# Softmax attention of a two-layer kernel: VectorE takes the maximum of a pair of products ahead of the low part of the weights in each slot

## The chip, the cores and the metric

The program runs on one core of a Trainium2 chip. The metric is the device time of one execution in microseconds (us), as the median over the runs. The profile is of one execution on that core.

## What is computed

The reference chains a linear attention, a mixture of 16 experts, a softmax attention and a mixture of 64 experts over two sequences of 2048 tokens of 256 features, all in float32. The change touches the softmax attention alone. Cut to that:

```python
h = layernorm(x); c_q, c_kv = h @ w_down_q.T, h @ w_down_kv.T
q, k, v = (heads of c_q @ w_up_q.T, c_kv @ w_up_k.T, c_kv @ w_up_v.T)   # 2 x 16 heads, 2048 x 64
q, k = rope(q), rope(k)
scores = jnp.einsum('bhqd,bhkd->bhqk', q, k) / 8
attn = jax.nn.softmax(scores, axis=-1)
out = jnp.einsum('bhqk,bhkd->bhqd', attn, v)
```

## The kernel before

The stages run one after the other, with a barrier between them; `softmax_attention` is one of them. It works through 32 heads (16 pairs of two), each in 32 **slots**. Slot n of a head is a quarter of the queries (512) against 256 keys. Eight slots (`PER`) make one quarter of the queries.

Operands of TensorE are float32 numbers in a rounded format (fp32r). To keep accuracy, each factor is split into a high and a low part. So there are these pieces of work, each with its own engine and its own queue, whose order is written out by hand:

- **TensorE** (`head`, from L1644), in slot n: first the *scores* of slot n+2 (4 matmuls, L1621 and L1622), then the *products* of slot n+13 (2 matmuls into `ps_u`, L1606; `PAHEAD` is 13), then the *values* of slot n (6 matmuls, L1638 to L1640, twice three). Products are a first look at the scores of a later slot, only for their maximum. They wait until the maximum before has been read out of `ps_u` (semaphore `u_max`), since there is one buffer. The values of slot n wait for the low parts of slot n (`pl_ready` from VectorE for the first half of the tile, `pl2_ready` from GpSimd for the second).
- **ScalarE** takes the exponential of the scores twice, into `pf` (float32, L1572) and `ph` (rounded, L1573).
- **GpSimd** (`low_part`, L1440) takes `pl = pf - ph` for the second half of each tile, and in slots 16 to 23 of a head splits the next head's values (`vh` L1427, `vl` L1433, in turn).
- **VectorE** takes `pl = pf - ph` for the first half (`low_part`, L1503), takes the maximum over the pair of products (`maxima`, L1485), and once in 8 slots, after the maximum of slots 2, 10, 18 and 26, makes the softmax's stabilising row of a quarter of the queries (`stabilisers`, L1490, L1495 and L1497, all of four elements per partition). In slots 7, 9, 11 and 13 it also splits q and k of the next head: a bit mask (`cut_low`, L1471) ahead of the maximum and a subtraction (`take_low`, L1478) behind it. The last head has no head after it, so it splits nothing.

VectorE's low part in slot n is that of slot n+1, and its maximum that of slot n+13. Below, L(k), M(k), G(k) and V(k) stand for VectorE's low part, its maximum, GpSimd's low part and the start of the values of slot k. GpSimd's G(k+1) and VectorE's L(k+1) are both released by the same exponential of slot k+1.

The waits of the parts:

```python
dve.wait_ge(s["p_ready"], g * SLOTS + (n + 3))        # low_part(g, n): exponential of slot n
dve.wait_ge(s["u_full"], base * SLOTS + (j + 1))      # maxima: products of slot j
pe.wait_ge(s["u_max"], base * SLOTS + j)              # products: the maximum before
pe.wait_ge(s["pl_ready"], g * SLOTS + (n + 1))        # values, first half
```

Of the kernel before, what the change touches and what calls it, by code (L numbers as in the profile page):

```python
# [133 lines left out]
class Kernel:  # L134
# [1145 lines left out]
    def softmax_attention(self):  # L1280
# [3 lines left out]
        SLOTS = NQB * KC // 2  # L1284
# [7 lines left out]
        with ctx:  # L1292
# [172 lines left out]
            @block.vector  # L1465
            def _(dve):
                def cut_low(base, hh, half, i):

                    if i == 0:
                        dve.wait_ge(s[f"raw{hh}"], half * 32 + 32)  # L1470
                    dve.tensor_scalar(cut[:, i % 2], raw[hh][:, i * QB:(i + 1) * QB].bitcast(U32), KEEP, None,  # L1471
                                      ALU.bitwise_and).then_inc(s["cut_ready"], 1)

                def take_low(base, hh, i):
                    dve.wait_ge(s["cut_ready"], base * NQB + (i + 1))
                    if i > 1 or not isinstance(base, int) or base > 0:
                        dve.wait_ge(s[f"low{i % 2}"], base * 64 + 32 * (i // 2))
                    dve.tensor_tensor(low[:, i % 2], raw[hh][:, i * QB:(i + 1) * QB].bitcast(F32),  # L1478
                                      cut[:, i % 2].bitcast(F32), ALU.subtract).then_inc(s["low_ready"], 1)

                def maxima(base, hh, j):

                    qb, i = j // PER, j % PER
                    dve.wait_ge(s["u_full"], base * SLOTS + (j + 1))
                    dve.tensor_reduce(mx[:, qb % 2, 2 * i:2 * i + 2], ps_u[:], X, ALU.max).then_inc(s["u_max"], 1)  # L1485

                def stabilisers(base, hh, j):
                    qb = j // PER
                    dve.wait_ge(s["u_max"], base * SLOTS + (j + 1))
                    dve.tensor_reduce(mg[:], mx[:, qb % 2].rearrange("p (t k) -> p t k", k=4), X, ALU.max)\  # L1490
                        .then_inc(s["mg_ready"], 1)
                    if not isinstance(base, int) or base > 0:
                        dve.wait_ge(s[f"row{qb}"], base * 32)
                    dve.wait_ge(s["mg_ready"], base * NQB + (qb + 1))
                    dve.tensor_scalar(nmh[:, qb], mg[:], -1.0, None, ALU.mult).then_inc(s["own"], 1)  # L1495
                    dve.wait_ge(s["own"], base * NQB + (qb + 1))
                    dve.scalar_tensor_tensor(nml[:, qb], mg[:], -1.0, nmh[:, qb].bitcast(F32), ALU.mult, ALU.subtract)\  # L1497
                        .then_inc(s["nm_ready"], 1)

                def low_part(g, n):  # L1500
                    dve.wait_ge(s["p_ready"], g * SLOTS + (n + 3))
                    at = slice(0, QB)
                    dve.tensor_tensor(pl[:, n % NP, at], pf[:, n % NP, at], ph[:, n % NP, at].bitcast(F32), ALU.subtract)\  # L1503
                        .then_inc(s["pl_ready"], 1)

                def head(pr, hh, prepare):
                    g = pr * 2 + hh
                    nxt = pr * 2 + (hh + 1)
                    for n in range(SLOTS):
                        if n + 1 < SLOTS or prepare:  # L1510
                            low_part(g, n + 1)
                        i = n - 7
                        cutting = prepare and 0 <= i < 2 * NQB and i % 2 == 0
                        if cutting:
                            cut_low(nxt, 1 - hh, pr + hh, i // 2)
                        j = n + PAHEAD
                        if j < SLOTS:
                            maxima(g, hh, j)
                        elif prepare:
                            maxima(nxt, 1 - hh, j - SLOTS)  # L1520
                        if cutting:
                            take_low(nxt, 1 - hh, i // 2)
                        if j % PER == PER - 1:
                            if j < SLOTS:
                                stabilisers(g, hh, j)
                            elif prepare:
                                stabilisers(nxt, 1 - hh, j - SLOTS)

                dve.wait_ge(s["fixed"], 4)
                for i in range(NQB):  # L1530
                    cut_low(0, 0, 0, i)
                    take_low(0, 0, i)
                for j in range(PAHEAD):
                    maxima(0, 0, j)
                    if j % PER == PER - 1:
                        stabilisers(0, 0, j)
                low_part(0, 0)
                for pr in range(PAIRS - 1):
                    head(pr, 0, True)
                    head(pr, 1, True)  # L1540
                head(PAIRS - 1, 0, True)
                head(PAIRS - 1, 1, False)

# [288 lines left out]
```

## Time and profile before

| | |
|---|---|
| time, median of 3 runs | 5355.44 us (5354.14 to 5355.58) |
| the profiled execution's own time | 5353.76 us |
| its span | 5351.6 us |
| TensorE busy in the span | 4242.4 us (79%) |
| VectorE | 3795.4 us (71%) |
| GpSimd | 2569.8 us (48%) |
| ScalarE | 2514.5 us (47%) |
| mean granted clock of TensorE | 0.887 |

The profiled execution's own time is 2.2 us longer than its span, and 1.7 us under the median. Shares of the span average over stages with different limits, so they do not say what bounds the attention. The attention's values run from 1355.7 us to 4265.5 us of the span, over half of it. A busy TensorE is not TensorE at its peak: matmuls overlap, so a gap between two starts can be hidden in their lengths, and the distance between starts is the better measure.

### The profile page before, as it was taken

What the parts mean: (1) busy time and instruction counts of PE and PEld (TensorE: products, weight loads), DVE (VectorE), ACT (ScalarE), POOL (GpSimd) and SP (SyncE); (2) the same over time, 40 slices, a digit from 0 to 9 for tenths busy, and PEclk for the clock granted to TensorE, in tenths of its full rate; (3) what the DMA queues carried; (4) which work ended last, traced back from release to release, by engine and by line L of the source; (5) the groups of instructions that cost most, each with busy time, mean ns of one, the idle gap of its engine ahead of it and who ended that gap; (6) DMA issues with size and microseconds to landing.
All of it is one profiled execution on the core that took longest, in us unless ns stands there. A gap on an engine that the chain in (4) does not pass through costs nothing. (4 is left out here: it accounts for less than half of the span.)

```text
span 5351.6 us, 60841 instructions
## 1 busy us (share of the span) xinstructions
PE 4242.4 (79%) x17953; PEld 3145.6 (59%) x17954; DVE 3795.4 (71%) x5546; ACT 2514.5 (47%) x3236; POOL 2569.8 (48%) x2320
## 2 busy tenths in 40 slices
PE   7963577674999999999999999999999845411274
PEld 5652243353777777777777777777777734311132
DVE  6755344474899999999999999999999712355322
ACT  2211111232677777777777777777777600000011
POOL 0003466365455555555555555555555500166664
PEclk8875899787999999999999999999999967755597
DMA  9022223366223232322223232323232166300366
GB/s 96 11 82 76 34 46 46 118 237 195 56 50 70 50 70 50 69 50 60 58 51 67 46 71 48 70 50 70 50 70 50 32 110 102 94 11 11 76 186 182
DMA packets 489984, 397.34 MB, mean 74 GB/s; under 512 B 225145, under 2 KB 428174, under 8 KB 477216
## 3 DMA queue, kind: packets, MB, share of 16 engines
q1 hardware_dynamic: 456992, 369.14, 30.7%
q0 software_dynamic: 32768, 25.44, 3.0%
q8 instruction: 113, 1.85, 0.1%
q14 instruction: 111, 0.91, 0.1%
HBM read 247.83 MB, written 116.75 MB: 68 GB/s over the span
## 5 line engine op out<-in xcount | busy, mean ns | idle before, releaser
L1440 POOL TENSOR_TENSOR at_pl<-at_pf,at_ph 128x512 fp32r<-128x512 f32 x1024 | 1430.1, 1397 | 1307.6 <-ACT at_ph L1573 1307.5
L1572 ACT ACTIVATE at_pf<-at_ps_s 128x1024 f32<-128x1024 f32 x1024 | 1051.4, 1027 | 789.4 <-PE at_ps_s L1622 786.6
L1485 DVE TENSOR_REDUCE at_mx<-at_ps_u 128x2 f32<-128x1024 f32 x1024 | 1243.1, 1214 | 156.8 <-PE at_ps_u L1606 156.8
L1503 DVE TENSOR_TENSOR at_pl<-at_pf,at_ph 128x512 fp32r<-128x512 f32 x1024 | 1202.1, 1174 | 71.5 <-ACT at_ph L1573 68.7
L1573 ACT ACTIVATE at_ph<-at_ps_s 128x1024 fp32r<-128x1024 f32 x1024 | 1046.9, 1022 | 0.0
L1622 PE MATMUL at_ps_s<-at_q,at_k 66*128 66x512 f32 x2048 | 818.4, 400 | 0.0
L1638 PE MATMUL at_ps_v<-at_ph,at_vh 128*128 128x512 f32 x2048 | 815.1, 398 | 0.2 <-POOL at_pl L1440 0.2
L1621 PE MATMUL at_ps_s<-at_q,at_k 128*128 128x512 f32 x2048 | 813.1, 397 | 0.3 <-ACT at_ph L1573 0.3
L1640 PE MATMUL at_ps_v<-at_pl,at_vh 128*128 128x512 f32 x2048 | 811.8, 396 | 0.0
L1639 PE MATMUL at_ps_v<-at_ph,at_vl 128*128 128x512 f32 x2048 | 803.6, 392 | 0.0
L730 POOL DMA_INDIRECT table<-rt_entry,rt_slot x320 | 316.9, 990 | 988.6 <-DVE rt_entry L626 521.8
L1606 PE MATMUL at_ps_u<-at_k,at_qp 128*128 128x512 f32 x2048 | 668.9, 408 | 68.9 <-DMA at_q<-at_low 45.3
L1606 PEld LDWEIGHTS at_ps_u<-at_k,at_qp 128*128 128x128 f32 x2048 | 373.3, 191 | 227.1 <-DVE at_mx L1485 107.2
L1622 PEld LDWEIGHTS at_ps_s<-at_q,at_k 66*128 66x128 f32 x2048 | 387.8, 189 | 94.8
L1640 PEld LDWEIGHTS at_ps_v<-at_pl,at_vh 128*128 128x128 f32 x2048 | 385.8, 188 | 97.1
L1621 PEld LDWEIGHTS at_ps_s<-at_q,at_k 128*128 128x128 f32 x2048 | 388.4, 190 | 91.5 <-ACT at_ph L1573 1.0
L1639 PEld LDWEIGHTS at_ps_v<-at_ph,at_vl 128*128 128x128 f32 x2048 | 384.4, 188 | 93.7
L1638 PEld LDWEIGHTS at_ps_v<-at_ph,at_vh 128*128 128x128 f32 x2048 | 385.0, 188 | 85.5 <-POOL at_pl L1440 0.6
L713 PE MATMUL rt_ps_p<-rt_mask,tri 128*128 128x16 bf16 (+1 forms) x64 | 13.7, 214 | 431.3 <-DVEq L606 313.2
L1723 PE MATMUL op_ps_o<-op_wo,op_oT 128*128 128x256 f32 x512 | 180.2, 528 | 188.5 <-DVE x_sb L1740 143.2
L713 PEld LDWEIGHTS rt_ps_p<-rt_mask,tri 128*128 128x128 bf16 x64 | 6.7, 104 | 456.3 <-DVEq L606 331.3
L1723 PEld LDWEIGHTS op_ps_o<-op_wo,op_oT 128*128 128x128 f32 x512 | 138.7, 278 | 230.0 <-DVE op_oT L1734 200.5
(217 smaller groups left out, 5230.7 us busy)
## 6 DMA issues: line engine op xcount, KB each, us to landing
at_k<-kT SPq DMA_DIRECT2D x64, 512.0 KB
at_q<-qT SPq DMA_DIRECT2D x64, 512.0 KB
ex_wgu<-Wgu_in SPq DMA_DIRECT2D x64, 384.0 KB
qT<-pj_rot SPq DMA_DIRECT2D x32, 512.0 KB, 3.1
vT<-pj_vo SPq DMA_DIRECT2D x32, 512.0 KB, 4.4
kT<-pj_rot SPq DMA_DIRECT2D x32, 512.0 KB, 3.1
at_raw<-qT SPq DMA_DIRECT2D x32, 512.0 KB, 4.7
at_raw<-kT SPq DMA_DIRECT2D x32, 512.0 KB, 6.6
```

Source lines behind the costliest of these rows:

```text
L1440: pool.tensor_tensor(pl[:, n % NP, at], pf[:, n % NP, at], ph[:, n % NP, at].bitcast(F32), ALU.subtract).then_inc(s["pl2_ready"], 1)
L1485: dve.tensor_reduce(mx[:, qb % 2, 2 * i:2 * i + 2], ps_u[:], X, ALU.max).then_inc(s["u_max"], 1)
L1503: dve.tensor_tensor(pl[:, n % NP, at], pf[:, n % NP, at], ph[:, n % NP, at].bitcast(F32), ALU.subtract)\
L1572: act.activation(pf[:, n % NP], ps_s[:, n % 2], ACT.Exp, scale=DH ** -0.5)
L1573: act.activation(ph[:, n % NP], ps_s[:, n % 2], ACT.Exp, scale=DH ** -0.5)\
L1606: m = pe.matmul(ps_u[:, w], tile, k1[hh][:, kb * QB:(kb + 1) * QB], start=True, stop=True)
L1621: pe.matmul(out, k1[hh][:, ks], q1[hh][:, qs], start=True, stop=False)
L1622: m = pe.matmul(out, k2[hh][0:MROW + 2, ks], q2[hh][0:MROW + 2, qs], start=False, stop=True)
L1638: pe.matmul(out, vh[:, hh, c], ph[:, n % NP, keys], start=c == 0, stop=False)
L1639: pe.matmul(out, vl[:, hh, c], ph[:, n % NP, keys], start=False, stop=False)
L1640: m = pe.matmul(out, vh[:, hh, c], pl[:, n % NP, keys], start=False, stop=c == KC - 1)
L1723: m = pe.matmul(ps_o[:, r % 2, 0:D], oT[:, r, g], wo[:, g], start=g == 0, stop=g == G - 1)
```

## The change

The two lines that issue VectorE's low part of the next slot move from the head of the slot to behind the maximum. No instruction is added or removed, and no wait is changed. Of the other instructions of a slot, the bit mask (L1471) stays ahead of the maximum, and the subtraction (L1478) and the stabilising row stay behind, now behind the low part too.

```diff
                     for n in range(SLOTS):
-                        if n + 1 < SLOTS or prepare:
-                            low_part(g, n + 1)
                         i = n - 7
                         cutting = prepare and 0 <= i < 2 * NQB and i % 2 == 0
                         if cutting:
...
                             maxima(g, hh, j)
                         elif prepare:
                             maxima(nxt, 1 - hh, j - SLOTS)
+                        if n + 1 < SLOTS or prepare:
+                            low_part(g, n + 1)
                         if cutting:
                             take_low(nxt, 1 - hh, i // 2)
                         if j % PER == PER - 1:
```

VectorE's queue, slots 7, 8 and 9 of the second head, before:

```order
L1503 TENSOR_TENSOR at_pl<-at_pf,at_ph 128x512
L1471 TENSOR_SCALAR at_cut<-at_raw 128x512
L1485 TENSOR_REDUCE at_mx<-at_ps_u 128x2
L1478 TENSOR_TENSOR at_low<-at_raw,at_cut 128x512
L1503 TENSOR_TENSOR at_pl<-at_pf,at_ph 128x512
L1485 TENSOR_REDUCE at_mx<-at_ps_u 128x2
L1503 TENSOR_TENSOR at_pl<-at_pf,at_ph 128x512
L1471 TENSOR_SCALAR at_cut<-at_raw 128x512
L1485 TENSOR_REDUCE at_mx<-at_ps_u 128x2
L1478 TENSOR_TENSOR at_low<-at_raw,at_cut 128x512
```

The same three slots after the change:

```order
L1471 TENSOR_SCALAR at_cut<-at_raw 128x512
L1485 TENSOR_REDUCE at_mx<-at_ps_u 128x2
L1503 TENSOR_TENSOR at_pl<-at_pf,at_ph 128x512
L1478 TENSOR_TENSOR at_low<-at_raw,at_cut 128x512
L1485 TENSOR_REDUCE at_mx<-at_ps_u 128x2
L1503 TENSOR_TENSOR at_pl<-at_pf,at_ph 128x512
L1471 TENSOR_SCALAR at_cut<-at_raw 128x512
L1485 TENSOR_REDUCE at_mx<-at_ps_u 128x2
L1503 TENSOR_TENSOR at_pl<-at_pf,at_ph 128x512
L1478 TENSOR_TENSOR at_low<-at_raw,at_cut 128x512
```

The low part of slot n+1 has moved behind the mask and the maximum, and stands directly ahead of the subtraction.

VectorE's queue, slot 18 and the start of slot 19 of the second head, before:

```order
L1503 TENSOR_TENSOR at_pl<-at_pf,at_ph 128x512
L1485 TENSOR_REDUCE at_mx<-at_ps_u 128x2
L1490 TENSOR_REDUCE at_mg<-at_mx 128x4
L1495 TENSOR_SCALAR at_nmh<-at_mg 128x4
L1497 SCALAR_TENSOR_TENSOR at_nml<-at_mg,at_nmh 128x4
L1503 TENSOR_TENSOR at_pl<-at_pf,at_ph 128x512
L1485 TENSOR_REDUCE at_mx<-at_ps_u 128x2
```

The same place after the change:

```order
L1485 TENSOR_REDUCE at_mx<-at_ps_u 128x2
L1503 TENSOR_TENSOR at_pl<-at_pf,at_ph 128x512
L1490 TENSOR_REDUCE at_mg<-at_mx 128x4
L1495 TENSOR_SCALAR at_nmh<-at_mg 128x4
L1497 SCALAR_TENSOR_TENSOR at_nml<-at_mg,at_nmh 128x4
L1485 TENSOR_REDUCE at_mx<-at_ps_u 128x2
L1503 TENSOR_TENSOR at_pl<-at_pf,at_ph 128x512
```

Behind the three small instructions of the row now comes a maximum, where a low part came before. TensorE's queue is the same in both kernels, and so are those of the other engines.

## Rows read from the trace of the kernel before

**Rows 1.** Busy time and clock, by stretch: the whole attention.

```profile
core 0: us, PE busy (x) PEld busy (x) DVE busy (x) ACT busy (x) POOL busy (x), PEclk, DMA share, GB/s
1355.00:4267.00 2912.00, 2903.55 (x12251) 2293.70 (x12249) 2682.28 (x2663) 2162.48 (x2296) 1641.16 (x1271) 1.00 0.25 56
```

**Rows 2.** TensorE in time, slot 7 of the 15th head.

```profile
start us, us, engine line op out<-in xcount [idle before <-releaser]
...
2652.94 0.39 PE L1621 MATMUL at_ps_s<-at_q,at_k 128*128 128x512 f32 x1
2653.17 0.40 PE L1622 MATMUL at_ps_s<-at_q,at_k 66*128 66x512 f32 x1
...
2653.88 0.63 PE L1606 MATMUL at_ps_u<-at_k,at_qp 128*128 128x512 f32 x2
2654.35 0.40 PE L1638 MATMUL at_ps_v<-at_ph,at_vh 128*128 128x512 f32 x1
```

**Rows 3.** The values' line L1638 from the 15th head's start to the 16th's.

```profile
L1638 PE MATMUL at_ps_v<-at_ph,at_vh x65: 391/397/400, 2634.7 to 2725.9; 128*128 128x512 f32 x65
```

**Rows 4.** The page's costliest groups: maximum, both low parts.

```profile
L1440 POOL TENSOR_TENSOR at_pl<-at_pf,at_ph 128x512 fp32r<-128x512 f32 x1024 | 1430.1, 1397 | 1307.6 <-ACT at_ph L1573 1307.5
...
L1485 DVE TENSOR_REDUCE at_mx<-at_ps_u 128x2 f32<-128x1024 f32 x1024 | 1243.1, 1214 | 156.8 <-PE at_ps_u L1606 156.8
L1503 DVE TENSOR_TENSOR at_pl<-at_pf,at_ph 128x512 fp32r<-128x512 f32 x1024 | 1202.1, 1174 | 71.5 <-ACT at_ph L1573 68.7
```

**Rows 5.** VectorE in time, the 15th head's slots 1 and 2 and behind.

```profile
2636.40 0.69 DVE L1503 TENSOR_TENSOR at_pl<-at_pf,at_ph 128x512 fp32r<-128x512 f32 x1 [0.29 <-ACT at_ph L1573]
2637.70 1.23 DVE L1485 TENSOR_REDUCE at_mx<-at_ps_u 128x2 f32<-128x1024 f32 x1 [0.60 <-PE at_ps_u L1606]
...
2642.24 1.23 DVE L1497 SCALAR_TENSOR_TENSOR at_nml<-at_mg,at_nmh 128x4 fp32r<-128x4 f32 x1
2643.40 0.68 DVE L1503 TENSOR_TENSOR at_pl<-at_pf,at_ph 128x512 fp32r<-128x512 f32 x1
2644.00 1.21 DVE L1485 TENSOR_REDUCE at_mx<-at_ps_u 128x2 f32<-128x1024 f32 x1
2645.13 1.67 DVE L1503 TENSOR_TENSOR at_pl<-at_pf,at_ph 128x512 fp32r<-128x512 f32 x1
```

**Rows 6.** GpSimd in time, the 15th head's slots 0 to 9.

```profile
2636.55 1.70 POOL L1440 TENSOR_TENSOR at_pl<-at_pf,at_ph 128x512 fp32r<-128x512 f32 x1 [1.10 <-ACT at_ph L1573]
...
2642.16 1.29 POOL L1440 TENSOR_TENSOR at_pl<-at_pf,at_ph 128x512 fp32r<-128x512 f32 x1 [1.10 <-ACT at_ph L1573]
2644.97 1.28 POOL L1440 TENSOR_TENSOR at_pl<-at_pf,at_ph 128x512 fp32r<-128x512 f32 x1 [1.51 <-ACT at_ph L1573]
...
2653.39 1.29 POOL L1440 TENSOR_TENSOR at_pl<-at_pf,at_ph 128x512 fp32r<-128x512 f32 x1 [1.49 <-ACT at_ph L1573]
2656.20 1.28 POOL L1440 TENSOR_TENSOR at_pl<-at_pf,at_ph 128x512 fp32r<-128x512 f32 x1 [1.51 <-ACT at_ph L1573]
2659.01 1.28 POOL L1440 TENSOR_TENSOR at_pl<-at_pf,at_ph 128x512 fp32r<-128x512 f32 x1 [1.52 <-ACT at_ph L1573]
```

**Rows 7.** Who waited for VectorE's maximum, L1485.

```profile
  PEld at_ps_u L1606: 107.2, 231
```

**Rows 8.** VectorE in time, slots 7 to 9 of the 15th head.

```profile
2655.16 0.41 DVE L1471 TENSOR_SCALAR at_cut<-at_raw 128x512 uint32<-128x512 uint32 x1
2655.49 1.21 DVE L1485 TENSOR_REDUCE at_mx<-at_ps_u 128x2 f32<-128x1024 f32 x1
2656.63 1.40 DVE L1478 TENSOR_TENSOR at_low<-at_raw,at_cut 128x512 fp32r<-128x512 f32 x1
```

**Rows 9.** VectorE in time, two neighbours that meet GpSimd, in another head.

```profile
1558.71 0.69 DVE L1503 TENSOR_TENSOR at_pl<-at_pf,at_ph 128x512 fp32r<-128x512 f32 x1 [0.29 <-ACT at_ph L1573]
1559.32 1.52 DVE L1471 TENSOR_SCALAR at_cut<-at_raw 128x512 uint32<-128x512 uint32 x1
```

**Rows 10.** GpSimd in time, the same stretch.

```profile
1558.86 1.70 POOL L1440 TENSOR_TENSOR at_pl<-at_pf,at_ph 128x512 fp32r<-128x512 f32 x1 [0.99 <-ACT at_ph L1573]
```

**Rows 11.** Lines with shapes kept apart: GpSimd's split of the values' low part.

```profile
L1433 POOL TENSOR_TENSOR at_vl<-at_vf,at_vh 128x256 fp32r<-128x256 f32 x124 | 134.3, 1083 | 0.0
```

## The prediction

> **What bounds the kernel now.** I first read the busy time by stretch: in the attention TensorE is busy 2903.55 of 2912 us at a granted clock of 1.00, the upper of its two levels (2.4 GHz) [rows 1]. The chain of waits has nothing to say of this stage, so I went to the order of instructions in time. In [rows 2] the starts of neighbouring matmuls are 0.23 us apart, and from the first scores' matmul (2652.94) to the values (2654.35) there are six of them in 1.41 us, 0.235 each. The reader is to see that this is TensorE's own pace: no gap is left. A slot has 12 matmuls; the values of slot 0 to slot 7 of that head start from 2634.7 [rows 3] to 2654.35, so 2.81 us a slot. I take 2.805.
>
> Then I looked for what lies above this pace. From one head's first value matmul to the next's it is 2725.9 - 2634.7 = 91.2 us [rows 3], while 32 slots of 2.805 are 89.8. So **1.4 us a head are lost to stalls**, some 45 us over 32 heads: this is all that any reordering in this stage can win. The waits name the loser: the weight load of the products waits for VectorE's maximum 231 times, 107.2 us in sum [rows 7]. (Some of that is hidden, since weights load ahead of time.)
>
> Why is VectorE late, at 1.21 us for a maximum and 0.69 for a low part, in a slot of 2.8? Because the low part takes 1174 ns on average, not 690 [rows 4]. The two timelines side by side show it. At 2636.40 L starts, G starts behind it at 2636.55 and takes 1.70, until 2638.25, which is 1.16 after L's end [rows 5, 6]. At 2644.97 G is first and takes its own 1.28; L, started at 2645.13, ends at 2646.80, 0.55 behind G [rows 5, 6]. So two subtractions of these engines do not run together: **the one that starts second ends 0.56 us behind GpSimd, or 1.15 us behind VectorE**. The maximum, which reads PSUM, is never held: 1214 ns on average [rows 4]. The tiny L1497 is held too: 1.23 us at 2642.24, until GpSimd's end at 2643.45 [rows 5, 6].
>
> **The change, step by step.** Instructions, durations and semaphores are the same; only who meets whom changes, and what the values wait for. I give times from V(n), the start of values in slot n.
>
> *A quiet slot.* G(n+2) starts at V(n)+1.85: 2656.20 against 2654.35 [rows 2, 6]. The maximum of slot n+13 can start at V(n)+0.20 (2637.70 [rows 5] against 2634.7+2.8) and takes 1.21 to 1.23. So the low part of slot n+1, now behind it, starts at V(n)+1.35 (neighbours overlap by 0.08, as 2643.40 + 0.68 and 2644.00 in [rows 5]) and ends at V(n)+2.04. It is needed at V(n)+2.805: on time by 0.75. It also starts 0.50 ahead of GpSimd, and GpSimd has 2.8 us until its half is needed, so that being held costs it nothing. A quiet slot stays at TensorE's pace, and gain and loss there are zero. What covers this is that half microsecond.
>
> *When the maximum starts more than 0.50 late.* Then G is first. It ends at V(n)+1.85+1.29, the low part 0.56 later, the values start some 0.06 behind: V(n)+3.76 in place of V(n)+2.805. **Each such low part costs TensorE 0.95 us**, a step and not a slope. The old order had the low part done a whole slot ahead, so only the maximum's own lateness cost anything.
>
> *Slots 7 to 9.* I walk the new queue in the times of the 15th head. L(7) runs 2652.87 to 2653.56; G, released at 2653.39 [rows 6], waits and ends at 2653.56 + 1.15 = 2654.71. The mask (0.41 alone [rows 8]) asks at 2653.48 and is held until 2655.00. The maximum follows, 2654.92 to 2656.13, and L(8) starts at 2656.05, before G at 2656.20 [rows 6]: in time, ends 2656.74. G now ends at 2657.89. The subtraction L1478 stands directly behind L(8), and is held until 2657.89 + 0.56 = 2658.45. The maximum of slot 8 could have started at 2657.35 and starts at 2658.37, over a microsecond late, and ends at 2659.58: products wait 0.15. L(9) comes at 2659.50, behind G at 2659.01 [rows 6], and ends at 2659.01 + 1.29 + 0.56 = 2660.86. V(9) was due at 2654.35 + 2 x 2.805 = 2659.96 and starts near 2660.92. Stall: 0.96 in all.
>
> *That GpSimd gets in between* is the link that decides. The trace has it: L starts at 1558.71 [rows 9], G at 1558.86 [rows 10]; the mask asks at 1559.32 with no gap behind L [rows 9], and yet G ends at 1560.56 [rows 10], 1.16 behind L, and the mask only at 1560.84 [rows 9].
>
> *The other slots.* The stall gives VectorE 0.95 us, and the backlog builds again. In slot 10 the row's small instructions are held by G(12), the mask of slot 11 comes behind them, its maximum starts 0.92 late, and L(12) meets G: 0.95 at slot 12. The same happens behind the mask and subtraction of slot 13, at L(15), by a margin of only 0.12 us. In slots 16 to 23 GpSimd also splits values, 1083 ns for the low part of a piece [rows 11]; in slot 18 L1497 is held by it, the maximum of slot 19 starts 0.3 late and slot 20's low part misses G by 0.26: a fourth stall. In slots 2 and 26 the row's instructions cost the next maximum some 0.3, under the 0.50: no stall.
>
> Sum: 4 x 0.95 = 3.8 us a head, less the 1.4 of today, whose cause (low parts held in a row, then a late maximum) mostly goes. That is +2.4 us in 31 heads (the last one splits nothing): **+73 us**. Against the profiled execution's own 5353.76 that is 5427; it lies 1.7 under the median, so 5428. Bounds: with the two sure stalls alone (slots 9 and 12) the sum is 1.9 - 1.4 = +0.5 a head, +15 us, 5370; with a fifth, 4.75 - 1.4 = +3.35, +104 us, 5459. I take four, since the walk finds four, the nearest rows being those of the same slots.
>
> The rows give 0.55 between GpSimd's end and that of a held low part whose free length is 0.69, so a part of the work goes on while it is held. The Trainium skill (SBUF — State Buffer, section "SBUF: two separate sides" and the one behind it) has VectorE and GpSimd share a port pair that the first holds for its whole instruction while the other fully blocks, and gives about 115 ns on top of the other's end before the blocked one runs. Taken at its word, a late low part would end 0.69 + 0.115 behind G, some 0.25 later than by the rows, which over 4 x 31 is 30 us more, 5458 (an estimate from that page and these counts). Rows come first.
>
> **Rivals.**
>
> 1. *Faster, 5312.* VectorE keeps its place against GpSimd between neighbours, and the backlog disappears. Without GpSimd in between, L1478 of slot 7 would end at 2657.35, the maximum of slot 8 would start on time at 2657.35, and L(9) at 2658.48, ahead of G at 2659.01. All 1.4 us of today's stalls would go as well, since low parts at 0.69 in place of 1174 ns [rows 4] free VectorE: 31 x 1.4 = 43 us less. It decides if the low part's start stays under V(n)+1.85. For it speaks that quiet slots are surely better off; against it [rows 9, 10]. 9%.
> 2. *No change.* The stalls only change hands: one new stall of 0.95 and some short ones in place of the 1.4. It needs the mask of slot 7 or the subtraction not to be held. 5350 to 5365. 5%.
> 3. *Slower, but by little.* Two stalls a head: the later ones hang on margins of 0.12 and 0.26. 5370 to 5395. 20%.
> 4. *The forecast*, three to five stalls: 5400 to 5460. 64%, and 2% for more.
>
> **How the numbers follow.** The measurement can tell about 0.2%, 11 us. Faster is rival 1, 0.09; same is rival 2, 0.05; the rest, 0.86, is slower. The predicted time is that of the likeliest case, 5428. The range takes in cases 3 and 4, 5370 to 5460.
>
> **What would show it.** In the changed profile: maxima as long as before (1.21), low parts shorter on average (about 0.85 us), GpSimd's longer; TensorE's values at L1638 now wait for VectorE's low part L1503, which is nearly absent today, about 4 times a head near slots 9, 12, 15 and 20 with gaps of 0.8 to 0.95; the products' waits for the maximum nearly gone; one head at 93 to 94 us in place of 91.2. The forecast is wrong if the low part at slot 9 starts ahead of GpSimd's, or if a head takes 90 us. Stages ahead of 1355 us and behind 4267 us must not move.

## The result, and the profile after

The change makes the kernel slower: 5444.59 us (median of 4 runs, 5442.53 to 5447.85) against 5355.51 us (4 runs, 5354.14 to 5355.82). The ratio is 1.0167, with a 95% interval of 1.015 to 1.0185; that is 89 us more.

The busy time of the attention, with its columns as in [rows 1], and the page's costliest groups, as in [rows 4], after the change:

```profile
1354.00:4350.00 2996.00, 2910.29 (x12251) 2285.07 (x12249) 2415.12 (x2663) 2163.94 (x2295) 1550.01 (x1271) 1.00 0.25 54
```

```profile
L1440 POOL TENSOR_TENSOR at_pl<-at_pf,at_ph 128x512 fp32r<-128x512 f32 x1024 | 1381.8, 1349 | 1483.5 <-ACT at_ph L1573 1483.4
L1485 DVE TENSOR_REDUCE at_mx<-at_ps_u 128x2 f32<-128x1024 f32 x1024 | 1249.7, 1220 | 565.3 <-PE at_ps_u L1606 565.0
...
L1503 DVE TENSOR_TENSOR at_pl<-at_pf,at_ph 128x512 fp32r<-128x512 f32 x1024 | 904.0, 883 | 19.4 <-ACT at_ph L1573 19.4
L1638 PE MATMUL at_ps_v<-at_ph,at_vh 128*128 128x512 f32 x2048 | 831.0, 406 | 85.7 <-DVE at_pl L1503 85.5
```

The attention is 84 us longer at the same granted clock of 1.00, and VectorE is busy there for 267 us **less** than in [rows 1]: its low part takes 883 ns in place of 1174. An average like this would speak for the change. The last row is what costs: TensorE's values now wait for VectorE's low part, 85.5 us in sum, a line that before had no such entry. That this sum is so near the loss is chance. It counts the idle time alone, 0.70 us at each of 122 waits, while the starts of the values move by 0.94 us there and by another 0.10 in the next slot: 129 us in all, from which the 44 us of the old stalls go. The maximum costs less in exchange: the products' weight load waits for it 104 times in place of 231, 49.7 us in sum in place of 107.2.

```profile
  PEld at_ps_u L1606: 49.7, 104
```

One head, the 15th, from its first value matmul to the next head's (the values' line, as in [rows 3]), and who waits for VectorE's low part over the whole run:

```profile
L1638 PE MATMUL at_ps_v<-at_ph,at_vh x65: 390/397/503, 2671.0 to 2765.0; 128*128 128x512 f32 x65
```

```profile
who waited for it (us, times):
  PEld at_ps_v L1638: 156.0, 216
  PE at_ps_v L1638: 85.5, 122
```

94.0 us a head in place of 91.2, and 122 waits of TensorE: four in each of the 31 heads that have one after them would be 124. In this head they are at slots 9, 12, 15 and 20, by the distances between the starts of values: 3.75 us in place of 2.81 at each.

Now the place where it happens. VectorE, GpSimd and TensorE in time, slots 7 to 9 of that head (columns: start, duration, engine, instruction, idle time before it in brackets):

```profile
2689.14 0.68 DVE L1503 TENSOR_TENSOR at_pl<-at_pf,at_ph 128x512 fp32r<-128x512 f32 x1
2689.74 1.52 DVE L1471 TENSOR_SCALAR at_cut<-at_raw 128x512 uint32<-128x512 uint32 x1
2691.18 1.21 DVE L1485 TENSOR_REDUCE at_mx<-at_ps_u 128x2 f32<-128x1024 f32 x1
2692.31 0.68 DVE L1503 TENSOR_TENSOR at_pl<-at_pf,at_ph 128x512 fp32r<-128x512 f32 x1
2692.91 1.78 DVE L1478 TENSOR_TENSOR at_low<-at_raw,at_cut 128x512 fp32r<-128x512 f32 x1
2694.61 1.21 DVE L1485 TENSOR_REDUCE at_mx<-at_ps_u 128x2 f32<-128x1024 f32 x1
2695.74 1.36 DVE L1503 TENSOR_TENSOR at_pl<-at_pf,at_ph 128x512 fp32r<-128x512 f32 x1
```

```profile
2689.65 1.32 POOL L1440 TENSOR_TENSOR at_pl<-at_pf,at_ph 128x512 fp32r<-128x512 f32 x1 [1.49 <-ACT at_ph L1573]
2692.46 1.68 POOL L1440 TENSOR_TENSOR at_pl<-at_pf,at_ph 128x512 fp32r<-128x512 f32 x1 [1.49 <-ACT at_ph L1573]
2695.27 1.29 POOL L1440 TENSOR_TENSOR at_pl<-at_pf,at_ph 128x512 fp32r<-128x512 f32 x1 [1.13 <-ACT at_ph L1573]
```

```profile
2695.88 0.73 PE L1606 MATMUL at_ps_u<-at_k,at_qp 128*128 128x512 f32 x2
2697.16 0.50 PE L1638 MATMUL at_ps_v<-at_ph,at_vh 128*128 128x512 f32 x1 [0.55 <-DVE at_pl L1503]
2697.50 0.40 PE L1639 MATMUL at_ps_v<-at_ph,at_vl 128*128 128x512 f32 x1
2697.74 0.39 PE L1640 MATMUL at_ps_v<-at_pl,at_vh 128*128 128x512 f32 x1
```

The low part of slot 8 (2692.31) is ahead of GpSimd's (2692.46) by 0.15 us. The subtraction behind it is held (1.78 in place of 0.68), the next maximum is late, and slot 9's low part (2695.74) comes 0.47 behind GpSimd's start (2695.27). It ends at 2697.10, and the values start at 2697.16. The last two rows show something the prediction did not have: from the late matmul to the next are 0.34 us and not 0.23.

### The profile page after: what moved, and what is told of

The parts are those of the page before. It is cut to its first block and busy times, and to the rows that moved or that the text cites. A ratio compares the mean times of both kernels' runs of the same rounds, so it can differ in the third digit from the quotient of the medians.

```text
span 5445.8 us, 60841 instructions
## 1 busy us (share of the span) xinstructions
PE 4257.3 (78%) x17953; PEld 3142.5 (58%) x17954; DVE 3528.5 (65%) x5546; ACT 2517.0 (46%) x3236; POOL 2478.2 (46%) x2320
## 5 line engine op out<-in xcount | busy, mean ns | idle before, releaser
L1440 POOL TENSOR_TENSOR at_pl<-at_pf,at_ph 128x512 fp32r<-128x512 f32 x1024 | 1381.8, 1349 | 1483.5 <-ACT at_ph L1573 1483.4
L1485 DVE TENSOR_REDUCE at_mx<-at_ps_u 128x2 f32<-128x1024 f32 x1024 | 1249.7, 1220 | 565.3 <-PE at_ps_u L1606 565.0
L1503 DVE TENSOR_TENSOR at_pl<-at_pf,at_ph 128x512 fp32r<-128x512 f32 x1024 | 904.0, 883 | 19.4 <-ACT at_ph L1573 19.4
L1638 PE MATMUL at_ps_v<-at_ph,at_vh 128*128 128x512 f32 x2048 | 831.0, 406 | 85.7 <-DVE at_pl L1503 85.5
L1606 PE MATMUL at_ps_u<-at_k,at_qp 128*128 128x512 f32 x2048 | 655.3, 401 | 61.0 <-DMA at_q<-at_low 45.1
L1638 PEld LDWEIGHTS at_ps_v<-at_ph,at_vh 128*128 128x128 f32 x2048 | 384.6, 188 | 237.2 <-DVE at_pl L1503 156.0
L1606 PEld LDWEIGHTS at_ps_u<-at_k,at_qp 128*128 128x128 f32 x2048 | 384.2, 192 | 180.1 <-DVE at_mx L1485 49.7
```

The lines of the kernel that those rows point to most:

```text
L1440: pool.tensor_tensor(pl[:, n % NP, at], pf[:, n % NP, at], ph[:, n % NP, at].bitcast(F32), ALU.subtract).then_inc(s["pl2_ready"], 1)
L1606: m = pe.matmul(ps_u[:, w], tile, k1[hh][:, kb * QB:(kb + 1) * QB], start=True, stop=True)
L1638: pe.matmul(out, vh[:, hh, c], ph[:, n % NP, keys], start=c == 0, stop=False)
```

## The experiments

Four theories. **A**: the low part is late where VectorE's maximum starts over 0.50 us late, because GpSimd's low part is then first and holds it, a step of 0.95 us or more. **B**: VectorE has too much work around slots 7 to 15, and a low part behind the maximum is late whoever it meets. **C**: the new order costs something in every slot. **D**: lateness adds up smoothly, without a step. C and D come up at the runs that speak of them.

The kernels ran in two groups of four, on two chips, on which the kernel before took 5351.6 us (first group) and 5310.2 us (second group); each is compared with its own group. The expectations were written as times against 5355.5 us for the kernel before and 5444.6 us for the new order, so the difference to the kernel before is what counts. The new order itself was not run again in these groups; where a kernel is compared with it, its 89 us and its stretch are those of the first measurement. "Stretch" is the time from the first to the last start on the values' line. It was 2909.8 us before and is 2994.6 us after the change, and it is free of what the stages ahead and behind do.

| kernel | median, us | against before, us | ratio (95%) | stretch, us |
|---|---|---|---|---|
| new order, GpSimd waits for L(k-1) | 5325.19 | -26 | 0.9948 (0.9931 to 0.9964) | 2882.6 |
| old order, GpSimd waits for L(k) | 5304.3 | -47 | 0.9912 (0.9896 to 0.9929) | 2864.9 |
| new order, GpSimd narrow | 5303.77 | -48 | 0.9906 (0.989 to 0.9923) | 2864.1 |
| old order in slots 7 to 15 | 5380.1 | +29 | 1.0054 (1.0037 to 1.0071) | 2936.5 |
| new order, split one slot later | 5363.94 | +54 | 1.0101 (1.0084 to 1.0118) | 2962.7 |
| new order, tiny mask and subtraction | 5328.88 | +19 | 1.0031 (1.0021 to 1.0042) | 2929.4 |
| old order, GpSimd narrow (one run) | 5270.03 | -40 | none | 2865.9 |
| new order, two added delays | 5415.3 | +105 | 1.0197 (1.018 to 1.0214) | 3011.4 |

### New order, with GpSimd's low part kept behind VectorE's

```diff
 def low_part(g, n):                       # GpSimd
     pool.wait_ge(s["p_ready"], g * SLOTS + (n + 3))
     stand_alone(pool, s["turns"])
+    if g * SLOTS + n > 0:
+        pool.wait_ge(s["pl_ready"], g * SLOTS + n)
+        stand_alone(pool, s["turns"])
```

> The new order, and GpSimd's low part of slot k starts only when VectorE's low part of slot k-1 is done, so that VectorE is never the second at the place where it came late. Theory A (the low part is late because it meets GpSimd's, which was first): the four stalls of 1.04 us a head shrink to two short ones, near slots 12 and 20, about 0.7 us a head in all; 5335 us. VectorE's low part then takes 0.69 us on average in place of 0.88. Theory B (VectorE has too much work in slots 7 to 15, and the low part behind the maximum is late whoever it meets): the added wait can only delay; 5445 us or more.

26 us faster than before, where 20 were expected, and so some 115 us faster than the new order without the wait. Adding a wait to GpSimd, and nothing else, took the loss away. Who waits for VectorE's low part now:

```profile
L1506 DVE TENSOR_TENSOR at_pl<-at_pf,at_ph x1024: 674/681/890, 1353.4 to 4236.9; 128x512 fp32r<-128x512 f32 x171
...
who waited for it (us, times):
  POOL at_pl L1443: 1373.5, 997
  PEld at_ps_v L1641: 21.2, 92
```

The longest low part is 890 ns, where it was 1779, and only weight loads wait, 21.2 us in sum. What is left are short stalls where they were expected: 0.23 us at slot 12 in most heads, and 0.39 us at slot 20 in 14 of them; 0.5 us a head in all, where 0.7 was said. Theory B, by which the wait could only delay, falls.

### Old order, with GpSimd's low part behind VectorE's

```diff
     stand_alone(pool, s["turns"])
+    pool.wait_ge(s["pl_ready"], g * SLOTS + (n + 1))
+    stand_alone(pool, s["turns"])
```

> The order of before, and GpSimd's low part of slot k starts only when VectorE's low part of the same slot is done. Theory A: VectorE is never held by GpSimd's low part, it keeps up in slots 7 to 15, and today's 1.4 us a head go: 31 x 1.4 = 44 us less, 5311 us, faster than both kernels. Theory B: VectorE's own work is what makes its maxima late, the time stays 5355 us or is longer by GpSimd's delay.

47 us faster than before, where 44 were expected. Of the kernels here that leave nothing out, this is the fastest.

```profile
L1505 DVE TENSOR_TENSOR at_pl<-at_pf,at_ph x1024: 682/693/956, 1348.0 to 4212.3; 128x512 fp32r<-128x512 f32 x171
its engine sat idle before it (us, times) until:
  ACT at_ph L1575: 241.4, 772
who waited for it (us, times):
  POOL at_pl L1442: 1444.4, 1024
```

```profile
L1640 PE MATMUL at_ps_v<-at_ph,at_vh x65: 397/400/400, 2607.1 to 2696.9; 128*128 128x512 f32 x65
```

The head takes 89.8 us, 32 slots of 2.805: TensorE's pace without a stall. GpSimd waits 1444.4 us for VectorE and it costs nothing, since its half is needed a slot later.

### New order, GpSimd's low part narrow

```diff
-    at = slice(QB, 2 * QB)
+    at = slice(QB, QB + 8)
```

> The new order, with GpSimd's low part cut to 8 of its 512 columns: the second half of each low part is left out of the values, so the output lacks that correction. Theory A: nobody holds VectorE, no stall is left, 5311 us. Theory B: the stalls of slots 9, 12, 15 and 20 stay, 5445 us.

48 us faster than before, where A gave 44; the stretch is 2864.1 us, the same as that of the kernel ahead within a microsecond. With GpSimd out of the way the new order has no stall, although VectorE's queue and the work in it are untouched.

### The change undone in slots 7 to 15

```diff
+    early = 7 <= n <= 15
+    if early:
+        low_part(g, n + 1)
...
-    if n + 1 < SLOTS or prepare:
+    if not early and (n + 1 < SLOTS or prepare):
         low_part(g, n + 1)
```

> The change undone in slots 7 to 15 of each head alone; the other slots keep the new order. Theory A: the stalls of 1.04 at slots 9, 12 and 15 go, short ones of the old order (about 1.0 us a head in all) take their place, and the stall at slot 20 stays: 2.1 us a head against 1.44 of before, 20 us above it, 5376 us. Theory C (the new order costs something in every slot): about a quarter of the 89 us goes, 5420 us.

29 us above before, and 60 of the 89 us are gone. The stretch is 26.7 us above before's. Theory C would have left most of the loss. TensorE waits for the low part 30 times, once a head:

```profile
who waited for it (us, times):
  PEld at_ps_v L1641: 41.1, 62
  PE at_ps_v L1641: 22.1, 30
```

The starts of the values put that one at slot 20 (0.94 late). In slots 8 to 15 the late maxima of the old order are back, 1.3 us a head, where I had said about 1.0; over 31 heads that is the 9 us by which the run is above the 20 expected.

### New order, the split of the values one slot later

```diff
-    i = n - SLOTS // 2
+    i = n - SLOTS // 2 - 1
```

> The new order, and GpSimd's split of the next head's values in slots 17 to 24 in place of 16 to 23, so that the piece that meets VectorE's small instructions of slot 18 is the short one (0.39 us) and not the subtraction (0.73 us). Theory A: the maximum of slot 19 then starts less than 0.5 us late, the low part of slot 20 is ahead of GpSimd's, and the stall at slot 20 is gone, 31 x 1.04 = 32 us less than the new order: 5412 us, or 57 us above before. Slots 9, 12 and 15 stay. Theory B (VectorE's work after the splitting of q and k drags on): nothing changes, 5445 us.

54 us above before (57 expected), a stretch 32 us shorter than with the new order alone (2962.7 against 2994.6). Slot 18 and the start of 19 in the 15th head:

```profile
2707.24 0.99 DVE L1495 TENSOR_SCALAR at_nmh<-at_mg 128x4 fp32r<-128x4 f32 x1
2708.26 0.30 DVE L1497 SCALAR_TENSOR_TENSOR at_nml<-at_mg,at_nmh 128x4 fp32r<-128x4 f32 x1
2708.48 1.21 DVE L1485 TENSOR_REDUCE at_mx<-at_ps_u 128x2 f32<-128x1024 f32 x1
2709.62 0.68 DVE L1503 TENSOR_TENSOR at_pl<-at_pf,at_ph 128x512 fp32r<-128x512 f32 x1
```

L1497 is held for 0.30 by the shorter piece, and the next low part (2709.62) is ahead of GpSimd's (2709.69), by 0.07 us, and not held. TensorE's waits for the low part fall from 122 to 92, one a head fewer. So the fourth stall hung on 0.34 us of GpSimd's work (0.73 against 0.39) met by a tiny instruction of the slot before the last.

### New order, tiny mask and subtraction

```diff
-    dve.tensor_scalar(cut[:, i % 2], raw[hh][:, i * QB:(i + 1) * QB].bitcast(U32), KEEP, None,
+    dve.tensor_scalar(cut[:, i % 2, 0:8], raw[hh][:, i * QB:i * QB + 8].bitcast(U32), KEEP, None,
```

and the same for the subtraction L1478 (L1479 in this kernel).

> The new order, with the bit mask and the subtraction that split q and k of the next head cut to 8 of 512 columns (the rest of the low parts of q and k is left out as zeros). VectorE has some 1.0 us less of its own work in each of slots 7, 9, 11 and 13, but both small instructions can still be held until GpSimd's end. Theory A: two stalls of 1.04 stay, at slots 12 and 20, 2.1 us a head against 1.44 of before: 20 us above before, 5376 us. Theory B (amount of work on VectorE): the stalls of slots 9, 12 and 15 all go, at most slot 20 stays: 5343 us or less.

19 us above before, 20 expected by A, 12 or more below it by B. TensorE waits 62 times, twice a head, and the starts of the values put these at slots 12 and 20:

```profile
  PE at_ps_v L1639: 46.3, 62
```

The stalls of slots 9 and 15 are gone, so there the length of the two instructions does count, as A too had it. With almost no work left in them, the third is still there: at slot 12 it is not VectorE's own work that is too long, but that small instructions stand in the queue and are held. In the 15th head the row's L1496 of slot 10, four elements, takes 1.00 us there. The subtraction over 8 columns, 0.15 us where nothing holds it, shows the same in its average:

```profile
L1479 DVE TENSOR_TENSOR at_low<-at_raw,at_cut 128x8 fp32r<-128x8 f32 x124 | 121.5, 980 | 0.0
```

### Old order, GpSimd's low part narrow

> The order of before, with GpSimd's low part cut to 8 of its 512 columns (that correction is left out of the values). Theory A: no stall, the time of the kernel with the new order and the same cut, 5304 us: without the meeting, the order of VectorE's two instructions is worth nothing. Theory B: the stalls of today's order stay, 5355 us.

One run, with the same edit as for the narrow part above: 5270.03 us where the kernel before had 5310.2 in that group, 40 us less, where some 50 were expected. The stretch, which leaves the other stages out, is 2865.9 us, within 2 us of that of the new order with the same cut. Without the meeting the order of the two instructions is worth nothing either way.

### New order, two added delays

```diff
     dve.wait_ge(s["u_full"], base * SLOTS + (j + 1))
+    if extra:
+        dve.tensor_reduce(junk[:, 0:1], self.C[:, 0:extra], X, ALU.max)
```

`extra` is 320 columns in slot 24, 640 in slot 29 and 0 elsewhere.

> The new order, with one added reduction on VectorE ahead of the maximum in two quiet slots of each head: over 320 columns in slot 24 (0.3 us) and over 640 columns in slot 29 (0.6 us). Nothing is left out. Theory A (a step at 0.50 us of lateness): the first costs nothing; the second lets GpSimd be first, and slot 30's values start 0.95 late plus 0.10 for the restart, 31 x 1.04 = 32 us above the new order: 5477 us. Theory D (lateness adds up smoothly): the low part is needed 0.75 us behind its end, so neither costs anything: 5445 us.

VectorE in time, the 15th head, slot 24 and slots 29 and 30:

```profile
2750.24 0.49 DVE L1487 TENSOR_REDUCE at_junk<-C 128x1 f32<-128x320 f32 x1 [0.97 <-PE at_ps_u L1609]
2750.64 1.22 DVE L1488 TENSOR_REDUCE at_mx<-at_ps_u 128x2 f32<-128x1024 f32 x1
2751.77 0.68 DVE L1506 TENSOR_TENSOR at_pl<-at_pf,at_ph 128x512 fp32r<-128x512 f32 x1
...
2764.16 0.82 DVE L1487 TENSOR_REDUCE at_junk<-C 128x1 f32<-128x640 f32 x1 [0.95 <-PE at_ps_u L1609]
2764.90 1.22 DVE L1488 TENSOR_REDUCE at_mx<-at_ps_u 128x2 f32<-128x1024 f32 x1
2766.03 1.68 DVE L1506 TENSOR_TENSOR at_pl<-at_pf,at_ph 128x512 fp32r<-128x512 f32 x1
```

GpSimd at the same two places:

```profile
2751.89 1.72 POOL L1441 TENSOR_TENSOR at_pl<-at_pf,at_ph 128x512 fp32r<-128x512 f32 x1 [1.48 <-ACT at_ph L1576]
...
2765.88 1.28 POOL L1441 TENSOR_TENSOR at_pl<-at_pf,at_ph 128x512 fp32r<-128x512 f32 x1 [1.52 <-ACT at_ph L1576]
```

The first delay moves the maximum by 0.40 us (2750.24 to 2750.64), leaves the low part 0.12 ahead of GpSimd, and costs nothing. The second moves it by 0.74, 0.34 more, and the low part is 0.15 behind GpSimd: it takes 1.68 and not 0.68, and slot 30's values start 0.98 late. TensorE's waits for the low part rise from 122 to 153, one more a head. So the step is there, between 0.40 and 0.74, and theory D falls. The added reductions were longer than I had said (0.49 and 0.82 in place of 0.3 and 0.6), so the second took nearly the whole reserve of 0.75, and this alone could have made it late by a few hundredths, not by 0.98.

The time is 105 us above before; by the new order's 89 and 32 it should be 121. The stretch shows the same: 3011.4 us, where 2994.6 and 32 make 3027. The difference lies in TensorE, not in the number of stalls: a quiet slot in this kernel is 2.79 us long in place of 2.805, which over 1024 slots is 15 us. Why that is stays open; no run was made for it.

## Why the prediction was right

**What bounds the stage.** TensorE's pace of 2.805 us a slot, with 1.4 us a head of stalls on top, was right to the last step: the best kernel takes 89.8 us a head, and 44 to 45 us is what could be won; 45 us of the stretch were.

**The quiet slot.** Right: low parts of 0.68 us, starting 0.51 us ahead of GpSimd's, and no stall. One sign that was given failed: GpSimd's low parts were to become longer, and their mean fell from 1397 to 1349 ns. In the old order it came 0.15 us behind VectorE's in quiet slots and took 1.70 us; coming 0.51 behind it takes 1.32, against 1.29 alone. Over 1.5 us it is 108 times now and was 255 times. Nothing in the sum hung on it.

**Who is first decides, and 0.50 us of lateness is the limit.** Right. That the order of arrival decides is shown by three kinds of run: GpSimd taken out of the way, GpSimd told to wait, and the maximum delayed by 0.40 and by 0.74. The changed kernel itself narrows the limit down. These are VectorE's and GpSimd's low parts at slot 15, in the 14th head and in the 15th:

```profile
2621.27 0.68 DVE L1503 TENSOR_TENSOR at_pl<-at_pf,at_ph 128x512 fp32r<-128x512 f32 x1
2621.27 1.83 POOL L1440 TENSOR_TENSOR at_pl<-at_pf,at_ph 128x512 fp32r<-128x512 f32 x1 [1.60 <-ACT at_ph L1573]
```

```profile
2714.31 1.73 DVE L1503 TENSOR_TENSOR at_pl<-at_pf,at_ph 128x512 fp32r<-128x512 f32 x1
2714.21 1.29 POOL L1440 TENSOR_TENSOR at_pl<-at_pf,at_ph 128x512 fp32r<-128x512 f32 x1 [1.50 <-ACT at_ph L1573]
```

In the 14th head VectorE is not behind: its low part is not held and slot 15 takes 2.80 us. In the 15th it is 0.11 behind, is held, and the slot takes 3.75. Seen from the 0.51 us of a quiet slot, the limit lies between 0.51 and 0.62 us of lateness.

**Slots 7 to 9.** The walk gave, from its V(7) of 2654.35, L(8) at 1.70 behind it, the next maximum at 4.02, L(9) at 5.15 until 6.51 and V(9) at 6.57. Measured, where V(7) started at 2690.60: 1.71, 4.01, 5.14 until 6.50, and 6.56. That GpSimd gets in between two neighbours of VectorE was the link that decided between the forecast and the rival on the faster side, and the subtraction of 1.78 us in the timeline shows it; this rival fell with it. It holds in all 92 places of the changed kernel's attention where GpSimd's low part came up during an instruction of VectorE and the mask or the subtraction stood directly behind: GpSimd's always ended first. The Trainium skill (SBUF — State Buffer, section "SBUF: two separate sides") has whoever is first keep the pair for the whole instruction, and the trace agrees. The figure that the prediction took from the section "A bandwidth-pool intuition that's wrong (but worth ruling out)", some 115 ns beyond the other's end, is measured there on DMA descriptors held up by VectorE, and it does not carry over: the low part ended 0.54 us behind GpSimd (2697.10 against 2696.56), not 0.80. The 30 us that this would have added were not there.

**Four stalls a head.** Right in number and place: slots 9, 12, 15 and 20, in 29 of the 31 heads; in the 14th the one of slot 15 is missing and in the 17th the one of slot 20, those with margins of 0.12 and 0.26 in the walk. These margins came out at 0.11 and 0.28. The walk was right to 0.02 us, but a count that hangs on 0.11 us is not a safe one: with slot 15 missing everywhere the loss would be some 32 us less.

**The sum, 73 us against 89 measured.** The term that was mis-sized is the price of a stall: 0.95 in the sum, 1.04 on the chip. The stall itself is 0.94, as walked; what the sum left out is 0.10 us in the next slot, the 0.34 in place of 0.23 from the late matmul to the next one. A full head is 4.2 us above the bare pace, not 3.8, and was 1.4 above it before; over the 31 heads that makes the 85 us of the stretch. The rest of the 89, 4 us, lies outside the attention, which the prediction said must not move. In the two profiled executions the time from the last value's start to the end of the span is 1096.5 us, where it was 1086.0; in the four kernels of the first group, in which those stages are unchanged too, it is 1084.3 to 1090.6. Executions of the kernel before alone, in that group, spread over 13 us. What makes the 4 us is not shown.

**The low part's average.** Said 0.85 us, measured 0.88. "Nearly gone" was too much for the products' waits for the maximum: their sum halved.

## What to carry to other kernels

Where two engines share something that one holds to the end of its instruction, look at who asks first and not at who is busy: here a subtraction cost 0.68 us or 1.7 us, and it was the order of arrival within 0.15 us that decided. Try to make the engine with reserve wait for the one without: here a wait on GpSimd, which had a slot of 2.8 us to spare, took 47 us off the kernel, while moving VectorE's instruction to a "better" place cost 89. And when an instruction is moved behind another, add up how late its new neighbour may start before it meets the next event, in every slot that carries extra work, and not in the quiet one alone.

## What was not expected of the hardware

- A wait that TensorE's matmul really stands in costs 0.10 us beyond the wait: 0.34 us to the next start in place of 0.23, in every one of the 122 stalls. Why is not shown.
- VectorE's instructions of four elements per partition can be held as long as large ones: L1495 took 0.99 us behind GpSimd, where it is 0.17 us alone.
- TensorE's slot was 2.79 us in one kernel and 2.805 in the others, at a granted clock of 1.00 in all of them.
